# A ring of 21 tiles instead of 20 in the middle part of a fused convolution kernel, with ScalarE's scratch and GpSimd's product in one buffer

## What is computed

```python
x = x + L0_conv(group_norm(x))          # layer 0: shift by fractions of a pixel, 1x1 conv
x = x + L1_conv(group_norm(x))          # layer 1:
    ll, lh, hl, hh = haar_dwt(x)                       # 4 x (8, 128, 128, 128)
    h = gelu(batchnorm(conv1x1(concat(ll, lh, hl, hh), w_c1, b_c1)))
    res = h
    o = dwconv3x3(h, dw_w, dw_b)                       # nine taps, per channel
    o = layernorm_chw(o, gn_g, gn_b)                   # mean and variance of a whole image
    o = conv1x1(gelu(conv1x1(o, pw1_w, pw1_b)), pw2_w, pw2_b)
    h = o + res
    h = gelu(batchnorm(conv1x1(h, w_c2, b_c2)))        # statistics over all eight images
    return haar_idwt(h)
```

## Time and profile before

| what | value |
|---|---|
| median of 3 runs | 5349.4 us (5344.71 to 5351.09) |
| the profiled execution | 5349.64 us, its span 5348.0 us |
| PE matmuls busy | 4636.7 us, 87% of the span |
| DVE busy | 4607.9 us, 86% |
| ACT busy | 4341.1 us, 81% |
| POOL busy | 1152.0 us, 22% |
| mean granted clock of TensorE | 0.962 |

### The profile page before, as it was taken

The page is one execution under the profiler, slowest core; times in us unless marked ns, Lnnn a source line. Parts: engine busy times, 40 slices in busy tenths (PEclk is TensorE's granted clock), DMA queues, the critical chain, the costliest instruction groups (busy, mean ns, idle before and its releaser), DMA issues. The chain is left out here.

```text
span 5348.0 us, 54815 instructions
## 1 busy us (share of the span) xinstructions
PE 4636.7 (87%) x12574; PEld 2144.3 (40%) x12574; DVE 4607.9 (86%) x4207; ACT 4341.1 (81%) x6467; POOL 1152.0 (22%) x855
## 2 busy tenths in 40 slices
PE   2789999999999999999998999999987777777775
PEld 1233334344343443444443666666642222222222
DVE  7999899898998989999907999999568888888887
ACT  5788888888888888888846888888578888888887
POOL 0000000000000000000005888888301111111111
PEclk7999999999999999999999999999999999999998
DMA  8999999999999999998972333333159999999999
GB/s 337 346 351 362 426 404 414 425 383 425 394 414 425 381 425 400 416 405 332 381 283 95 134 134 135 136 136 135 51 113 225 236 236 236 236 235 236 235 236 224
DMA packets 248866, 1542.05 MB, mean 288 GB/s; under 512 B 29424, under 2 KB 29808, under 8 KB 91504
## 3 DMA queue, kind: packets, MB, share of 16 engines
q1 hardware_dynamic: 156528, 936.14, 44.9%
q0 software_dynamic: 36864, 268.45, 24.2%
q10 hardware_dynamic: 55296, 335.57, 15.0%
HBM read 877.35 MB, written 662.70 MB: 288 GB/s over the span
## 5 line engine op out<-in xcount | busy, mean ns | idle before, releaser
L1142 PE MATMUL ps<-arena,c2T 128*128 128x512 f32 x2048 | 1024.3, 651 | 366.8 <-ACT arena L891 364.5
L963 PE MATMUL ps<-arena 128*128 128x512 f32 x2048 | 980.8, 623 | 40.2 <-DMA arena<-out_x 23.3
L941 PE MATMUL ps<-arena 128*128 128x512 f32 x2048 | 966.0, 598 | 45.1 <-DVE arena L1365 22.4
L936 PE MATMUL ps<-arena 128*128 128x512 f32 x1536 | 740.7, 605 | 79.7 <-DVE arena L1349 35.2
L1142 PEld LDWEIGHTS ps<-arena,c2T 128*128 128x128 f32 x2048 | 401.4, 205 | 989.0 <-ACT arena L891 559.7
L891 ACT ACTIVATE arena<-ps,small 128x512 f32<-128x512 f32 x1024 | 713.7, 778 | 98.6 <-DVE arena L1574 90.1
L1333 DVE SCALAR_TENSOR_TENSOR arena<-arena,shift 128x2048 f32<-128x2048 f32 x256 | 601.8, 2351 | 162.0 <-DMA arena<-in_x 100.9
L1458 DVE SCALAR_TENSOR_TENSOR ps<-arena,taps,ps 128x256 f32<-128x256 f32 (+1 forms) x604 | 655.8, 1133 | 19.6 <-PE ps L1087 19.0
L605 ACT ACTIVATE ps<-arena 128x1024 f32<-128x1024 f32 x512 | 526.4, 1028 | 159.8 <-ACT arena L642 146.9
L521 POOL TENSOR_SCALAR arena<-arena 128x256 f32<-128x256 f32 x112 | 103.9, 936 | 2518.8 <-DMA arena<-in_x 2387.3
L642 ACT ACTIVATE arena<-ps,small 128x1024 f32<-128x1024 f32 x512 | 565.0, 1104 | 91.1 <-PE ps L941 89.3
(11 more groups left out here) (169 smaller groups left out, 5907.7 us busy)
## 6 DMA issues: line engine op xcount, KB each, us to landing
arena<-in_x SPq DMA_DIRECT2D x508, 1024.0 KB, 14.4
out_x<-arena ACTq DMA_DIRECT2D x256, 1024.0 KB, 9.0
out_x<-arena POOLq DMA_DIRECT2D x256, 1024.0 KB, 17.0
arena<-out_x SPq DMA_DIRECT2D x208, 1024.0 KB, 16.7
y_dram<-arena ACTq DMA_DIRECT2D x128, 512.0 KB, 8.5
arena<-y_dram SPq DMA_DIRECT2D x128, 512.0 KB, 3.6
h_dram<-arena SPq DMA_DIRECT2D x112, 512.0 KB, 2.7
arena<-h_dram SPq DMA_DIRECT2D x112, 512.0 KB, 10.2
```

The source lines that it names most:

```text
L936: mm(ps[:, r, :], w_right[:, :], u_buf[k][:, 2 * r:2 * r + 2, 2:W + 2], start=False, stop=False, skip_group_check=True)
L941: last = mm(ps[:, r, :], w_center[:, :], v_buf[k][:, r * BANK:(r + 1) * BANK], start=False, stop=True, skip_group_check=True)
L963: last = mm(ps[:, 4 + s % 2, :], w_c1b[:, q, :], cells[:, q // 2, q % 2, :, :], start=(q == 0), stop=(q == 3))
L1142: last = mm(ps[:, 4 * k + q, :], c2T[:, q, :], h2[:, k * HC:(k + 1) * HC], start=True, stop=True)
```

## The change

It makes room for one tile more and shifts the old stage by one:

- RING 20 to 21, so OLD_LAG 19 to 20: tile 16 b enters pw1 two steps behind the norm step. HEAD 18 to 19.
- `pool_b` and `o_squares` are gone. ACT's product of tile t is written straight into `pool_sum[t % 2]`, POOL adds `pool_a` to it in place, `finish_o(t)` reads it, and then `square_o(t)` writes its squares over it (float32 now).
- `square_o` stands at the end of ACT's step for every tile: tile s-2 at the end of step s, not tile s-3 ahead of `put_tap(s)`. It still waits for the finish of its tile.
- `make_product(t)` waits for the square of t-2 instead of for POOL; POOL's first sum no longer waits for the finish of t-2.
- `w_pw1b` and `bias_pw1` are two each, by image; `o_weights` and `o_bias` no longer wait for the last tile of the image before.

```diff
-HEAD = 18
+HEAD = 19
-RING = 20
+RING = 21
...
-        o_squares = cut(TILE // 2).bitcast(BF16)
-        pool_a, pool_b = (cut(TILE) for _ in range(2))
-        w_pw1b = cut(P)
+        pool_a = cut(TILE)
+        w_pw1b = [cut(P) for _ in range(2)]
...
-                if t >= 2:
-                    pool.wait_ge(dw_acc, o_made(t - 2))
                 pool.wait_ge(pool_step, n + 1)
-                pool.tensor_tensor(pool_sum[t % 2], pool_a, pool_b, ALU.add).then_inc(pool_step, 1)
+                pool.tensor_tensor(pool_sum[t % 2], pool_a, pool_sum[t % 2], ALU.add).then_inc(pool_step, 1)
...
-                if t:
-                    act.wait_ge(pool_step, pool_done(t - 2) + 2)
-                nc.scalar.activation(rows(pool_b), h_tile(t, *POOL_TAPS[1]), ACT.Copy,
+                if t >= 2:
+
+                    act.wait_ge(o_squared, nth(t - 2))
+                nc.scalar.activation(rows(pool_sum[t % 2]), h_tile(t, *POOL_TAPS[1]), ACT.Copy,
...
-                nc.scalar.activation(o_squares, o_ring[t % RING], ACT.Square,
+                nc.scalar.activation(pool_sum[t % 2], o_ring[t % RING], ACT.Square,
...
-                if 0 <= s - 3 < TILES and (s - 3) % NT != NT - 1:
-                    square_o(s - 3)
...
-                if 0 <= s - 2 < TILES and (s - 2) % NT == NT - 1:
+                if 0 <= s - 2 < TILES:
                     square_o(s - 2)
...
-                dve.wait_ge(pw1_done, nth(b * NT - 1))
-                ts(w_pw1b[:, :], pw1T[:, :], ln_scale, None, ALU.mult).then_inc(w_ready, 1)
+                if b:
+                    dve.wait_ge(pw1_done, nth((b - 1) * NT - 1))
+                ts(w_pw1b[b % 2], pw1T[:, :], ln_scale, None, ALU.mult).then_inc(w_ready, 1)
...
-                dve.wait_ge(a_ready, nth(b * NT - 1))
-                tt(bias_pw1, ps_small_o[:, 4:5], bpw1[:, :], ALU.add).then_inc(ln_ready, 1)
+                if b:
+                    dve.wait_ge(a_ready, nth((b - 1) * NT - 1))
+                tt(bias_pw1[b % 2], ps_small_o[:, 4:5], bpw1[:, :], ALU.add).then_inc(ln_ready, 1)
```

More of the change, by code:

```diff
@@ L22 @@
 HELD = 6
-ARENA = 50960
+ARENA = 51300
 HC = CH // 4
@@ L86, in preact_kernel @@
         center_w, inv_center_y = shift[:, 6:7], shift[:, 7:8]
-        small = sb("small", [P, 40])
+        small = sb("small", [P, 42])
         mom = small[:, 0:2]
@@ L95, in preact_kernel @@
         q1, bias1, h_scale, h_bias = (small[:, k:k + 1] for k in range(13, 17))
-        ln_scale, ln_shift, bias_pw1, h2_mean = (small[:, k:k + 1] for k in range(17, 21))
+        ln_scale, ln_shift, _, h2_mean = (small[:, k:k + 1] for k in range(17, 21))
+        bias_pw1 = [small[:, k:k + 1] for k in range(40, 42)]
         z_mean, z_scale, z_bias = small[:, 21:25], small[:, 25:29], small[:, 29:33]
@@ L813, in make_a @@
                 nc.scalar.activation(a_buf, z_bank(q).rearrange("p a n -> p (a n)"), ACT.Gelu,
-                                     bias=bias_pw1).then_inc(a_ready, 1)
+                                     bias=bias_pw1[q // NT % 2]).then_inc(a_ready, 1)
             def copy_hT(q, half):
@@ L1038, in first_conv @@
                 for half in range(2):
-                    last = mm(z_bank(q)[:, half, :], w_pw1b[:, :], o_ring[q % RING][:, half * BANK:(half + 1) * BANK],
+                    last = mm(z_bank(q)[:, half, :], w_pw1b[q // NT % 2], o_ring[q % RING][:, half * BANK:(half + 1) * BANK],
                               start=True, stop=True)
@@ L1480, in o_moments @@
                 if b:
-                    dve.wait_ge(gram_done, nth((b * NT - 3) * 2))
+                    dve.wait_ge(gram_done, nth((b * NT + (NT + 2 - OLD_LAG - 2)) * 2))
                 nc.vector.memset(ps_small_o, 0.0)
```

## The result

| | before | changed kernel |
|---|---|---|
| median of 5 runs | 5346.99 us (5344.71 to 5351.09) | 5373.47 us (5371.37 to 5376.62) |
| ratio, 95% interval | | 1.0047 [1.0036, 1.0058] |
| span of the profiled execution | 5348.0 us | 5369.7 us |

The account below looks back on a forecast made before the run. It took PE and DVE as full in full steps, PE alone in head and tail. 15.1 + 8.0 - 1.1 = +22.0 us on 5349.64 gave 5371.4 us, with 8 in 10 for 5361 to 5384.

Parts of the forecast that it names:

- The head's loop: Head: h and product enter the loop square, put, taps, 4.87 to 7.04 us; eight tiles 1.89 late, +15.1 us.
- The first norm step: From PE's last taps before the norm to the first make_h2: 27.8 us in place of 19.84, +8.0.
- One full step less, one tail step more: Full steps and tail: -7.50 us for the full step, +6.41 for the tail step, -1.1 together.
- Full steps: Square's new place in full steps: fits ACT's 0.70 us gap, taken as 0, bounds 0 and +1.4 us.
- the prediction's list of signs: Expected in the profile: head's finish_o starts alternating, later first make_h2, full steps 7.50 to 7.53, one more tail step.
- The boundaries and POOL's waits: Later boundaries: new weights 0, at best -5.8 us; blocked small adds at eight norms 0, 6.4 at most either way.
- The head hides it: Rival, chance 0.12: ACT's order not binding, head keeps 5.15 us a tile, +4.1, 5353.5 us.
- The clock falls in the pauses: Rival, chance 0.10: PE's clock drops in the head's new pauses, 6 to 12 us more, 5377 to 5384.
- Faster: Rival, chance 0.05: the boundaries were the bound and their waits go, giving 5336 us.

Follow-up runs that it names:

- e3: Kernel before, with only the first image's squares (tiles 0 to 15) at the end of ACT's step: 5369.32 us, ratio 1.0031.
- e1: Changed kernel with ACT's old order in the head (h, square of s-3, put, product): 5360.73 us, ratio 1.0017.
- e5: Changed kernel with put_tap(s) ahead of product(s-1) in the head, square left at the end of the step before: 5367.41 us in one run.
- e8: Changed kernel plus eleven matmuls that nothing reads, filling PE's idle time at the first norm step: 5372.2 us in one run.
- e6: Kernel e1 with HEAD 18 in place of 19, so tile 18 is an ordinary tile again: 5349.65 us in one run.
- e4: Kernel before, with squares at the end of ACT's step from tile 15 on only, head as it was: 5351.7 us, ratio 1.0003.
- e2: Kernel before, with every square at the end of ACT's step, its own buffers, ring and weights kept: 5366.29 us, ratio 1.0033.
- e9: Kernel e4 with ACT's product moved behind the gelu: 5362.04 us in one run.

## Why the prediction was right, point by point

The middle part grew by 27.2 us where 22.0 were forecast. That the time, 5373.47, lies only 2.1 over the forecast 5371.4 is luck in part: the forecast started from the median of three runs of before, 5349.4, and that of five is 5346.99.

**The head's loop: right.** +16.1 for +15.1. The mechanism, the eight waits, the alternating steps (5.15 and 7.14; 5.15 and 7.04 were said) and the cause are as foretold; e3, e1 and e5 show it: they make the loss, undo it and halve it. The difference is the 5.26 for 12 instructions behind a pause, eight times 0.1.

**The first norm step: right in sum (+7.6 for +8.0), by terms that offset each other.** To the start of the taps 5.44 (5.0 taken), the 12 instructions up to the next product 7.54 (6.9), from there to the start of finish_o(18) 6.45 (6.6), from that to the first make_h2 8.00 (9.3). The last is the clock: PE was back at 2.4 GHz for the second conv (1.98 us), where I had carried over the 3.68 of the earlier trace rows; the first conv took 3.41 where before it took 2.98. e8 adds that 3.7 of the 27.44 are the clock's, and e6 that the wait for `finish_o(18)`, which the sum had in it, is what makes the tile dear.

**One full step less, one tail step more: -0.1 for -1.1.** The full step is exact. The tail's is 7.44, not the 6.41 of the earlier trace rows: the added step lies beside the last norm, where three steps of before (9.14, 6.99, 7.56) became four (8.45, 8.71, 6.41, 7.57). e6 has the same 7.45.

**Full steps: the term that was mis-sized.** I took 0 for the square's new place, with +1.4 as the bound, and wrote that the second conv might start 0.2 later "once, not each step". It does so once per turn of the ring, since then ACT's list has the border row too and no pause left. I had weighed one step of ACT, not its fullest. That is +1.4 in the changed kernel and +1.5 in e4; with the boundaries, +3.55 and +4.2 in all. So full steps did not stay at 7.50 to 7.53, as the prediction's list of signs had it.

**The boundaries and POOL's waits: right that nothing is gained, and a hold more came in.** DVE's waits of 0.73 and 0.24 stayed, and PE still waits 1.30 us for the small product with pw1T. Of the bounds of 6.4 either way, 1.3 came true. Of the +0.72 in the next three intervals, 0.6 lie in two images. The 0.2 of one of them are in the step that ends with f(83), which is again a border row's place, 21 behind f(62); the other 0.4, around f(99), I did not settle.

**The rivals.** *The head hides it* was refuted by the eight waits. *The clock falls in the pauses* did not happen in the changed kernel: eight pauses of 1.7 to 2.2 us left it at 1.00, and 24 instructions took 10.57, 0.44 apiece. It is not ruled out for this head, though. Of four traces with the same eight pauses (the changed kernel, e2, e3, e8) that of e2 has it once, behind the last pause of 2.23, for 1.7 us. In the earlier trace rows one of 2.17 was followed by slow work too, and in e9 a second conv behind one of 1.94 took 3.48 us. So the length of a pause alone is not what decides; what does was not tried. *Faster* was refuted: no boundary became shorter by as much as 0.1 us.

## What to carry to other kernels

In an engine's list, what stands between an instruction that waits and the next one that others wait for belongs to their loop, even if it has its inputs long before. Work out that loop's length for each regime of the kernel: the same move cost 16 us in the head, where the margin was 0.28 us, and some 4 in the 96 steps behind it, of which the 66 full ones lost 1.4, at the fullest steps above all. When no engine is full after a change, look for the loop; undo the order alone before blaming buffers.

## What the runs showed of the hardware

- A DVE instruction on 128 x 1 that started behind a POOL instruction on 128 x 896 or 128 x 1024 took 0.98 to 2.12 us in place of 0.16 to 0.22, and ended with it. Moving POOL's work by 1.9 us cost 11 us over six boundaries (e9). A DVE instruction with one input was held as well: L1482 of the changed kernel took 0.42 (its shortest is 0.17) and ended at 3310.75, POOL's L568 at 3310.72.
- Pauses of 1.7 to 2.2 us between groups of 10.6 us of matmuls, eight in a row, did not lower TensorE's clock in three traces of four; in e2 the last of them did (granted clock 0.75 over the 12 matmuls behind it, 7.11 us in place of 5.42). Idle times of 5.2 and 6.1 us at the norm step did: matmul groups there took 1.4 to 1.8 times as long, and small fillers took that back, 3.7 us in all (e8).
